# The diagonal matrix of a softmax maximum moves from VectorE to ScalarE

## What is computed

```python
def attention(k, v, q):                      # k = v = context, q = layernorm(x)
    kp, vp, qp = k @ Wk.T, v @ Wv.T + bv, q @ Wq.T + bq
    scores = qp @ kp.T / sqrt(512)
    probs = softmax(scores, axis=-1)         # subtracts each row's maximum
    return (probs @ vp) @ Wo.T + bo
x = x + attention(context, context, layernorm(x))
x = x + experts(layernorm(x))                # top 2 of 16, capacity 512, silu
```

## Time and profile before

| What | Value |
| --- | --- |
| median of 3 runs | 1712.02 us |
| lowest, highest run | 1711.95, 1714.20 us |
| the profiled execution's own time | 1715.9 us |
| its span, first to last instruction | 1714.2 us |
| mean granted TensorE clock | 0.966 |
| TensorE busy (matmuls) | 1602.2 us, 93% of the span |
| VectorE busy | 1177.3 us, 69% |
| GpSimd busy | 859.6 us, 50% |
| ScalarE busy | 718.9 us, 42% |

### The profile page before, as it was taken

The page is one execution under the profiler, slowest core; times in us unless marked ns, Lnnn a source line. Parts: engine busy times, 40 slices in busy tenths (PEclk is TensorE's granted clock), DMA queues, the critical chain, the costliest instruction groups (busy, mean ns, idle before and its releaser), DMA issues. The chain is left out here.

```text
span 1714.2 us, 41283 instructions
## 1 busy us (share of the span) xinstructions
PE 1602.2 (93%) x15821; PEld 1063.8 (62%) x15821; DVE 1177.3 (69%) x2271; ACT 718.9 (42%) x1060; POOL 859.6 (50%) x832
## 2 busy tenths in 40 slices
PE   8999989999999999999999999999997299999964
PEld 4444767766776677766777677766773145555530
DVE  4443276788887888788887888788875365555524
ACT  2443244445444444445444444445443144545430
POOL 0100055566655665566655665566656345656540
PEclk9999999999999999999999999999998599999985
DMA  4310111112111211212111211212110269899869
GB/s 160 93 44 13 51 26 45 51 45 50 45 45 45 55 40 45 51 46 49 45 45 45 54 41 45 51 45 50 45 38 20 61 181 225 201 225 200 182 108 372
DMA packets 202282, 140.39 MB, mean 82 GB/s; under 512 B 135010, under 2 KB 151394, under 8 KB 202148
## 3 DMA queue, kind: packets, MB, share of 16 engines
q1 hardware_dynamic: 179696, 94.27, 19.8%
q0 software_dynamic: 16896, 35.42, 11.0%
q10 hardware_dynamic: 5556, 8.66, 1.4%
HBM read 86.65 MB, written 51.68 MB: 81 GB/s over the span
## 5 line engine op out<-in xcount | busy, mean ns | idle before, releaser
L45 PE MATMUL sc<-qt,kT 128*128 128x128 f16 x3100 | 522.3, 219 | 3.4 <-POOL before L810 3.4
L47 PE MATMUL sc<-qt,kT 128*128 128x128 f16 x3100 | 522.3, 219 | 0.0
L46 PE MATMUL sc<-qt,kT 128*128 128x128 f16 x3100 | 522.3, 219 | 0.0
L45 PE MATMUL acc<-vv,pT 128*128 128x512 f16 x800 | 304.8, 381 | 4.4 <-DVE pT L1048 4.4
L45 PEld LDWEIGHTS sc<-qt,kT 128*128 128x128 f16 x3100 | 303.2, 98 | 7.4 <-POOL before L810 3.9
L46 PEld LDWEIGHTS sc<-qt,kT 128*128 128x128 f16 x3100 | 303.3, 98 | 3.5
L47 PE MATMUL acc<-vv,pT 128*128 128x512 f16 x800 | 304.8, 381 | 0.0
L46 PE MATMUL acc<-vv,pT 128*128 128x512 f16 x800 | 304.8, 381 | 0.0
L47 PEld LDWEIGHTS sc<-qt,kT 128*128 128x128 f16 x3100 | 303.3, 98 | 0.0
L856 POOL TENSOR_TENSOR sum<-sum,s_T 128x512 f32<-128x512 f32 (+1 forms) x160 | 281.9, 1762 | 26.4 <-ACT s_T L907 5.9
L896 ACT ACTIVATE s_T<-sc 128x512 f32<-128x512 f32 (+1 forms) x224 | 119.9, 548 | 259.9 <-PE sc L47 215.7
(11 more groups left out here) (296 smaller groups left out, 2822.6 us busy)
## 6 DMA issues: line engine op xcount, KB each, us to landing
xq<-in_x_dram SPq DMA_DIRECT2D x32, 256.0 KB, 2.6
x_in<-in_x_dram SPq DMA_DIRECT2D x32, 256.0 KB, 2.7
raw_g<-in_L_ffn_w_gate_dram SPq DMA_DIRECT2D x16, 512.0 KB
raw_f<-in_L_ffn_w_fc_dram SPq DMA_DIRECT2D x16, 512.0 KB
raw_p<-in_L_ffn_w_proj_dram SPq DMA_DIRECT2D x16, 512.0 KB
y_dram<-x SPq DMA_DIRECT2D x32, 256.0 KB, 2.0
rows_dram<-row SPq DMA_DIRECT2D x32, 256.0 KB
y_sb<-y_dram SPq DMA_DIRECT2D x16, 512.0 KB, 16.2
```

The lines of the kernel that those rows point to most:

```text
L45: pe.matmul(out, s_hi, m_hi, start=first, stop=False)
L46: pe.matmul(out, s_hi, m_lo, start=False, stop=False)
L47: return pe.matmul(out, s_lo, m_hi, start=False, stop=last)
```

## The change

On VectorE, the multiplication of the identity with `mx` in `shift` is taken out; the row maximum itself now raises a semaphore, `mx_rdy`. On ScalarE, a new function `diagonal(t)` waits for it and makes `diag` with an activation (a copy with the scale `mx`). It is called in `step` behind `tail_values(t)` and ahead of `rows_turned(t - 1)`, and once in the prologue ahead of the copies of tile 1's scores. `diag`, `spread` and everything else are as before.

```diff
+        mx_rdy = sem("mx_rdy")
...
+                def diagonal(t):
+                    act.wait_ge(mx_rdy, t + 1)
+                    act.activation(diag[:], ident[:], ACT.Copy, scale=mx[:]).then_inc(dg_rdy, 1)
+
...
                     if more:
                         tail_values(t)
+                        diagonal(t + 1)
                     if post:
                         rows_turned(t - 1)
...
                 for c in range(NCH):
                     copied(0, 0, c)
+                diagonal(0)
                 for c in range(3):
                     copied(1, 1, c)
...
                     dve.wait_ge(mx_pe, t + 1)
-                    dve.reduce_max(mx[:], ps_x[:, 0:P + TAIL], AX_X)
-                    dve.drain()
-                    dve.tensor_scalar(diag[:], ident[:], mx[:], None, ALU.mult).then_inc(dg_rdy, 1)
+                    dve.reduce_max(mx[:], ps_x[:, 0:P + TAIL], AX_X).then_inc(mx_rdy, 1)
+                    dve.drain()
                     wait_for(dve, pt_rdy, t)
                     dve.tensor_scalar(s_tail[:], ps_x[:, P:P + TAIL], mx[:], None, ALU.subtract).then_inc(st_rdy, 1)
```

## The result

The changed kernel takes 1696.12 us (median of 6 runs, 1693.63 to 1699.79) against 1713.37 us for the kernel before (6 runs, 1711.95 to 1718.07): a ratio of 0.9892, 95% interval 0.9877 to 0.9907. It is 1.1% faster; 1696 us was forecast.

The account below looks back on a forecast made before the run. TensorE was taken to bound the attention stage, with 18.7 us of stalls at `spread` to win; less 2.5 us remaining, 16.2 us off the 1712.0 median made 1696 us. Own range 1692 to 1700, full range 1692 to 1709.

Parts of the forecast that it names:

- TensorE's own interval: Attention stage: time from one `spread` to the next less TensorE's stalls there, put at 34.41 us.
- The moved steps: ScalarE's `rows_turned`, `tail_exp` and exponentials, now behind the wait for the maximum: costed at nothing, the copy covered by 3.6 us.
- The ring: Round of the engines other than TensorE in attention: 35.03 us, claimed not to go through `diag` while X1 comes first.
- X1: GpSimd's first addition of tail values (first L820) in a tile, behind bias add L816; forecast to start at 804.32.
- the two kinds: Attention tiles alternating before the change, with intervals between `spread`s of 35.2 and 34.8 us in turn.
- S1: VectorE's first subtraction of the next tile, forecast to start 0.23 us ahead of X1 and take 1.21 instead of 1.70.
- alternation: Attention tiles where S1 wins (ring 33.59 us) mixed with tiles where X1 wins (34.95), averaging 34.50 or 34.27.
- rival C: GpSimd starved in attention as subtractions go ahead of X1: slower, 11 us at two subtractions, 1723 us; chance 0.06.
- The residual stall: TensorE at `spread`: still up to 0.27 us every second or third tile, 2.5 us over 28 tiles.
- A: Rival: X1 still wins everywhere in attention, gaining 2 to 6 us, 1710 to 1706 us; chance 0.19.
- B: Rival: S1 wins, but half is given back at the copy for TensorE's sixth chunk: about 9 us, 1703; chance 0.14.
- D: Rival: no effect, ScalarE's wait for the maximum makes late behind it what it wins ahead: 1712 us; chance 0.04.

Follow-up runs that it names:

- experiment 1: Kernel before, with `diag` still made by VectorE but from a copy of the identity in PSUM: 1697.93 us, ratio 0.9892.
- experiment 2: Kernel before, with GpSimd's bias add (L816) moved ahead of the routing scatter: 1702.94 us, ratio 0.9921.
- Experiment 4: Changed kernel, with `diagonal` behind `rows_turned` on ScalarE instead of ahead of it: 1714.52 us, ratio 0.9993 to the kernel before.
- Experiment 3: Changed kernel, with `m_b` copied twice on VectorE: 1715.04 us, ratio 0.9995 to the kernel before.
- experiment 5: Changed kernel, with ScalarE's `diagonal` made twice, the first into an unused buffer: 1705.17 us, ratio 0.9934 to the kernel before.
- experiment 8: Changed kernel, with GpSimd's first addition of tail values held until VectorE's first subtraction is done: 1698.18 us, ratio 0.9902 to the kernel before.

## Why the prediction was right

- *The bound.* 18.7 us of stalls at `spread` were named as all that there is to win. All but 0.2 us of the stalls are gone and the stage is 18.5 us shorter. TensorE's own interval was put at 34.41 and is 34.40.
- *Why `diag` was late.* The hold by GpSimd's L816 is shown from two sides: with its source in PSUM (experiment 1) and with L816 elsewhere (experiment 2) the same instruction on VectorE takes 0.35 and 0.29 us.
- *`s_tail` isn't held up by L816.* It takes 0.22 us at 725.79 beside L817 (725.73 to 727.01).
- *`diag` on ScalarE.* 0.39 from the rows of copies, 0.403 measured. It starts 0.03 behind the maximum's end.
- *The moved steps* cost nothing at their covers: TensorE has no wait in the stage. Experiment 4 shows the other side: `rows_turned` could wait, `diag` could not.
- *The ring doesn't go through `diag` while X1 wins.* This was argued from one late tile in the trace. Experiment 3 shows it: a ring of 35.08 (where the two kinds alternate) with a `diag` of 0.40, against 35.03 with one of 1.31.
- *S1 wins.* It does, by 0.15 to 0.20 us (0.23 forecast). But it wins in **every** tile from the fifth to the last but one, where alternation was forecast: the step "the ring gains 1.44 us in such a tile" was mis-sized (its own rows, 806.76 less 805.30, make 1.46); it gained about 0.9 (35.03 to 34.1). S1's end did come 1.31 us earlier against the bias add (4.04 behind its start before, 2.73 after). Some 0.7 of that is given back before the next bias add. GpSimd's sums end no earlier, so more of VectorE's small instructions in `route` now run beside them and are held up. L1098 at 742.47, L1103 at 743.29 and L1116 at 743.97 take 0.50, 0.55 and 0.47 us, and the last two each end 0.03 behind an addition of GpSimd (743.08 to 743.81, 743.95 to 744.41). The same three in the tile of 804.15 before:

```profile
820.78 0.24 DVE L1092 SCALAR_TENSOR_TENSOR hit<-lg,m,rev 128x16 f32<-128x16 f32 x1
...
821.34 0.24 DVE L1097 TENSOR_SCALAR oh<-rev,r 128x16 bf16<-128x16 f32 x1
...
821.71 0.18 DVE L1110 SCALAR_TENSOR_TENSOR lg<-oh,lg 128x16 f32<-128x16 bf16 x1
```

That makes 0.87 us against this tile; everything of VectorE behind `route` is late by just that. In the kernel before it was the first of the three alone that was held up, in every second tile (14 of 64 instances of L1092 above 0.4 us, now 28 of 64), and those are the tiles with the interval of 35.2: this is a part of the two kinds, which the prediction had not traced. ScalarE's L930 also waits 0.28 for GpSimd. That is the mechanism of rival C, inside its bound. `diag` is ready 0.3 before `spread` is reached, so this ring is about 34.1 us and not 33.59. With 33.59 the maximum, the bias add and X1 would come 0.52 earlier against `spread`, X1 at 0.46 behind it instead of 0.98 and so ahead of S1 at 0.80 (an estimate), and the tiles would alternate as forecast. By this estimate it is the time given back that lets S1 win every time.
- *The residual stall* of 2.5 us is therefore 0.2. 16.2 us were forecast from the attention stage; it gave 18.5 in the profiled executions, and the medians moved by 17.3. That 1696 was met to 0.1 us is luck: the gain was 1.1 us larger than forecast, and the median of the kernel before, 1712.0 in the prediction, was 1.4 higher with the later runs. The other steps stood, and the regime that was described, S1 and X1 in turn with a stall of up to 0.3, is what experiment 2 shows in part of its tiles; experiment 5 has both orders too, with stalls of 0.13 and 0.70.
- *The rivals.* A (X1 wins, all but in a few tiles) is experiment 3's kernel and 4's, with 0.9995 and 0.9993; they gained 0.8 and 1.3 us, at or below the 2 to 6 us that it was priced at. B didn't occur. C occurs mildly, in `route`; a GpSimd that comes later still does no harm (experiment 8). D was refuted by the empty list of waits.

What stays open: why X1 starts 0.41 us behind L816 in the steady tiles while it is 0.32 in a late one. The prediction had put X1 at 0.32; it stayed at 0.41, and this 0.09 is about half of the margin that the gain rests on. Nor was it traced to a cause why three of the steady tiles before (X1 0.43 to 0.65 late, with a longer interval) and two after (1.57 and 1.68 behind `spread` instead of 1.0, harmless there, since S1 is on) have a late X1.

## What to carry to other kernels

Where TensorE stalls by a constant time each round, ask which ring of the other engines is that much longer than TensorE's own round; the instruction that it is seen to wait for need not be on that ring. Here the short `diag` counted only because it let one subtraction get to a shared resource up to 0.20 us before another engine; 0.37 us more at the copy ahead of it took the whole gain back, and 0.31 us more at `diag` half of it. So write down the margin along with the gain, or, as in experiment 8, fix the order with a semaphore. Before an instruction is moved to another engine, see whether it is slow or only held up: compare its minimum with its median, and look which engine's instruction it ends behind. If it is held up, moving its source to PSUM did the same here; moving the other engine's instruction made it as short but gave only 12.9 us, since that changed the race behind it too.

## What the runs showed of the hardware that was not expected

- The same VectorE instruction (128x128, float32, a scale from SBUF) takes 286 ns from SBUF when alone, 1308 beside a GpSimd addition, and 350 to 353 from PSUM beside the same addition. From PSUM it is slower by 65 ns and never held up.
- Tiny VectorE instructions that read SBUF are held up as well: 128x16 elements (L1098) take 0.41 to 0.51 us beside GpSimd's sums and 0.24 otherwise.
- Behind GpSimd's second scatter instruction, an addition with a drain ahead of it starts only 1.45 us later (experiment 2: 694.10, 695.54), though its inputs are there; behind an addition the pause is 0.2 to 0.4. What the 1.45 consists of, no run shows.
- Two engines whose instructions start 0.005 us or more apart are still served in the order of their starts (experiment 5; of two tiles with X1 ahead by 0.001 and 0.004, S1 won both), so the order can change by hundredths of a us.
